# Pass 0 of a five-pass graph network: eight comparisons with a per-row scalar become two comparisons of whole tensors

## The reference

```
x = layernorm(x + L0(x))   # h = relu([x[src], edge_attr] @ W1a + b1a); h @ W1b + b1b; mean over the edges of each target; two dense layers
x = layernorm(x + L1(x))   # sum of x[src] * rsqrt(deg_out[src]) over the edges of each target, * rsqrt(deg_in), dense, batch norm
x = layernorm(x + L2(x))   # mean of x[src] over the edges of each target, dense, elu
x = layernorm(x + L3(x))   # two weighted relational convolutions, 4 relations
```

## Time and profile before

| | us |
|---|---|
| Median of three runs | 4328.8 |
| Profiled execution, its own time | 4328.8 |
| Its span | 4327.0 |
| GpSimd busy in the span | 3052.1 (71%) |
| TensorE busy, matmul | 2871.7 (66%) |
| VectorE busy | 1770.1 (41%) |
| ScalarE busy | 803.5 (19%) |

### The profile page before, as it was taken

The page is one execution under the profiler, slowest core; times in us unless marked ns, Lnnn a source line. Parts: engine busy times, 40 slices in busy tenths (PEclk is TensorE's granted clock), DMA queues, the critical chain, the costliest instruction groups (busy, mean ns, idle before and its releaser), DMA issues.

```text
span 4327.0 us, 54093 instructions
## 1 busy us (share of the span) xinstructions
PE 2871.7 (66%) x18556; PEld 2377.0 (55%) x18556; DVE 1770.1 (41%) x6259; ACT 803.5 (19%) x1557; POOL 3052.1 (71%) x3155
## 2 busy tenths in 40 slices
PE   5999999999889997999844444444443333333333
PEld 5888888888767775666533333433332333333333
DVE  7888888888752226333411111111111222121221
ACT  1445444444431113112200000000000000000000
POOL 4777777777347773777467777777767777777776
PEclk8999999999999997999855555555555555555555
DMA  6666676666556764777422222222221111111111
GB/s 206 216 212 211 211 218 211 211 215 209 172 149 199 202 199 124 222 222 225 134 61 66 62 66 62 66 66 62 62 62 54 56 54 56 53 55 54 56 55 51
DMA packets 413092, 556.43 MB, mean 129 GB/s; under 512 B 67041, under 2 KB 287969, under 8 KB 412545
## 3 DMA queue, kind: packets, MB, share of 16 engines
q0 software_dynamic: 114112, 262.48, 21.2%
q1 hardware_dynamic: 277184, 264.23, 19.8%
q10 hardware_dynamic: 21506, 26.10, 1.8%
HBM read 450.01 MB, written 102.55 MB: 128 GB/s over the span
## 4 chain that ended last, share of the span: by engine, by line
POOL 21%; PE 14%; DMA 9%; issue 7%; ACT 0%; DVE 0%; POOLq 0%; ACTq 0%; DVEq 0%; SPq 0%
POOL work L528 21%; PE bank L1134 13%; DMA work<-table_rel,reli 9%; PE bank L1743 0%; DMA table_rel<-work 0%; ACT work L1755 0%; ACT work L1815 0%; PE bank L1792 0%; DVE X L1876 0%; POOLq L95 0%; PE bank L1741 0%; ACTq L1819 0%; POOLq L595 0%; DVE work L1166 0%; PE bank L1988 0%
## 5 line engine op out<-in xcount | busy, mean ns | idle before, releaser
L528 POOL DMA_INDIRECT work<-table_rel,reli x1664 | 1612.5, 969 | 573.0 <-issue 461.3
L1134 PE MATMUL bank<-work 128*128 128x72 f32 x3328 | 750.8, 419 | 1259.6 <-DMA work<-table_rel,reli 1259.6
L1134 PEld LDWEIGHTS bank<-work 128*128 128x128 f32 x3328 | 708.9, 324 | 1323.5 <-DMA work<-table_rel,reli 1323.5
L528 POOL DMA_INDIRECT work<-table_pre,srci x832 | 805.8, 968 | 269.7 <-issue 267.8
L1116 DVE TENSOR_TENSOR acc<-acc,bank 128x72 f32 x208 | 47.8, 230 | 1749.5 <-PE bank L1134 1749.5
L1062 PE MATMUL bank<-work,acc 128*128 128x360 f16 x2574 | 437.9, 317 | 30.3 <-DVE acc L1204 18.0
L764 PE MATMUL bank<-w1a,work 128*128 128x256 f32 x1664 | 441.3, 391 | 17.7 <-DVE work L729 8.7
L528 POOL DMA_INDIRECT work<-table_mean,srci x312 | 303.7, 973 | 168.7 <-issue 87.5
L776 PEld LDWEIGHTS bank<-work 128*128 128x128 f32 x3328 | 399.5, 194 | 6.9 <-ACT work L863 2.2
L776 PE MATMUL bank<-work 128*128 128x64 f32 x3328 | 401.0, 275 | 1.6 <-ACT work L863 1.5
L528 POOL DMA_INDIRECT work<-table_gcn,srci x312 | 295.9, 948 | 109.7 <-issue 94.8
(11 more groups left out here) (264 smaller groups left out, 3201.8 us busy)
## 6 DMA issues: line engine op xcount, KB each, us to landing
work<-adj SPq DMA_DIRECT2D x104, 720.0 KB
adj<-X SPq DMA_DIRECT2D x130, 450.0 KB
work<-ea_cols SPq DMA_DIRECT2D x208, 256.0 KB, 3.0
work<-adj SPq DMA_DIRECT2D x52, 810.0 KB
work<-table_rel,reli POOLq DMA_INDIRECT x1664, 2.5
work<-table_pre,srci POOLq DMA_INDIRECT x832
table_rel<-work ACTq DMA_DIRECT2D x25, 512.0 KB
table_rel<-work SPq DMA_DIRECT2D x25, 512.0 KB
```

The costliest lines, as they stand in the source:

```text
L528: pool.indirect_dma_start(into[:, u, :], None, tables[p], bass.IndirectOffsetOnAxis(ap=idx_of(p)[:, t:t + 1].bitcast(U32), axis=0)).then_i ...
L1134: mm = pe.matmul(bank[4 + n % LATE_BANKS][:, 0:PAIR_WIN], late_gat[n % LATE][:, u, :], late_hot[:, n % LATE_HOTS, u * PAIR_WIN:(u + 1) * P ...
```

## The change

In `one_hot`, the function that makes the three one-hots of a group in pass 0, the four comparisons for `hot` (L648) give way to a call of `one_hot_of`, which the other passes use: one comparison of 128x256, of the tensor `iota` with the tensor `local`. The four comparisons for `hot_hi` (L651) give way to one comparison of 128x200, of `iota` (32-bit, where it was the 16-bit `iota_b`) with `src_hi`. The four for `hot_lo` stay. What is written is the same.

```
-            for u in range(U):
-                dve.tensor_scalar(hot[:, hq, u * WIN:(u + 1) * WIN], iota[:, 0:WIN], local[:, bass.ds(g * U + u, 1)], None,
-                                  ALU.is_equal)
-            for u in range(U):
-                dve.tensor_scalar(hot_hi[:, hq, u, :], iota_b[:, 0:NT], src_hi[:, bass.ds(g * U + u, 1)], None, ALU.is_equal)
+            one_hot_of(dve, g, hot[:, hq, :])
+            dve.tensor_tensor(hot_hi[:, hq, :, :], iota[:, 0:NT].unsqueeze(1).broadcast_to([P, U, NT]),
+                              src_hi[:, bass.ds(g * U, U)].unsqueeze(2).broadcast_to([P, U, NT]), ALU.is_equal)
```

## The result

The kernel after takes 4352.2 us (4350.6 to 4355.0), the kernel before beside it 4329.6: ratio 1.0053, 95% interval 1.0039 to 1.0067. It is slower by 22.6 us. I had forecast 4336.8 (+8), with a range up to 4347.

The account below looks back on a forecast made before the run. The prediction took GpSimd's gather instruction time to bound pass 0, with VectorE able only to stretch gathers. Terms -0.5 + 8 + 0.5 = +8 us on 4328.8 gave 4336.8 us, range 4327 to 4347.

Parts of the forecast that it names:

- What bounds pass 0: Pass 0: everybody follows GpSimd's gathers, median 946 ns plus a 0.30 us gap; VectorE can move only 18.3 us of stretches.
- VectorE's own time: Pass 0: VectorE saves some 0.65 us a group, 135 us in the pass, hidden behind GpSimd; value 0.
- What leaves: Pass 0: gather stretch under the removed L648 and L651 goes; 0.5 us off, 9.0 us at most.
- The mechanism: A gather reads indices 0.13 us in; a two-SBUF-input instruction stops that read from about 0.15 us after its start to its end.
- What comes: Pass 0: the two new comparisons stretch gathers; equal chance gives 9.8 us, bounds 5 and 14, taken as 8.
- The stretches of L677 itself: Pass 0: a faster VectorE can only change the phase of the L677s; +0.5 us, bounds -3 and +4.
- The stages behind: Stages after pass 0 are only shifted and keep their length.
- Rival B: Pass 0: reads are stopped from a comparison's first moment, or the phases meet; +20 us, 4349; chance 0.1.
- A: Pass 0: the phases miss, so the comparisons stretch almost nothing; +1 to +3 us, 4331; chance 0.24 together with D.
- C: Pass 0: all one-input comparisons hold gathers, eight go and the two new ones miss; 9.0 us faster, 4319.8; chance 0.06.
- D: Pass 0: VectorE gets ahead of TensorE and L677 waits more for its buffer; 0 to +2 us, counted with A.
- The range: Whole kernel: 4327 to 4347 us, reaching to A below and half way to Rival B above; forecast's own 4333 to 4343.

Follow-up runs that it names:

- e4: Kernel after, but both new comparisons read their row of numbers from PSUM, with the wait for that bank moved ahead of them: 4329.8 us, ratio 0.9999.
- e4c: Control for e4: kernel after with only the earlier wait for the bank, the row still in SBUF: 4350.5 us, ratio 1.0051.
- e1: Kernel before with only the first half of the change, one 128x256 comparison for hot; the four for hot_hi stay: 4338.6 us, ratio 1.0022.
- e2: Kernel before with only the second half of the change, one 128x200 comparison for hot_hi; the four for hot stay: 4333.3 us, ratio 1.0013.
- e3c: Kernel after with hot_lo's four comparisons moved between the two new ones: 4340.0 us, ratio 1.0021.
- e11: Kernel before; in passes 3 and 4 the 128x576 comparison reads its row from the just-emptied PSUM bank, ordered add, multiplication, comparison: 4291.8 us, ratio 0.9909.
- e7c: Kernel before; in passes 3 and 4 the 128x576 comparison, in its old place, reads its row from PSUM after a wait for TensorE: 4340.1 us, ratio 1.0024.
- e5c: Kernel after with each group's code comparisons (L675) moved behind the next group's one-hots: 4351.4 us, ratio 1.0045.
- e6: e4 with each code comparison cut into two halves, eight in place of four: ratio 1.0007 beside a kernel before that took 5031 us.

## Why the prediction was wrong

It named the right place, the right mechanism for one instruction by itself and the right sign, and mis-sized one term by two: what the two comparisons cost, 8 us forecast and 15.5 measured. Another 3 us came where 0.5 was forecast, by the same omission.

*What bounds pass 0.* Right. GpSimd's median of 946 ns and its gap stayed; 17.8 us more busy time are the 17.9 us of the pass.

*VectorE's own time.* Right: 417 and 357 ns (420 and about 360), the busy time of the whole span down by 121 us (144), more wait for landings, 244 us (about 250), and all of it worth nothing.

*What leaves.* Right in size: -0.8 us (-0.5), though 0.35 of it is only the first gather, which in after is counted under L640.

*The mechanism.* The read at 0.13 us, the hold to the end of an instruction with two SBUF inputs: e4 against e4c shows it, and e1 and e2 pay the equal-chance price, 5.6 + 3.9 = 9.5 us for 9.8.

*What comes: the step that failed.* "I take 8: a little under equal chance, because the comparisons stand behind L729 and L677, and a gather that L677 has held back just before has its next read 1.25 us later, past both comparisons, which are over after 0.7 us." Measured were 15.5 us, above the upper bound of 14 too. Two things are wrong in the sentence. The first is its unspoken assumption that a read held by the first comparison is let in at its end: 18 reads under the first were handed on to the end of the second, 5.0 us (after), none when the two stand apart (e3c, with 9.2 us of stretch under the comparisons). Of the 15.5, 0.35 are the pass's first gather, 5.0 this hand-on, and the other 10.2 what equal chance gives (9.8). The second is the phase. 1.25 us are counted from the end of the L677 that held the read, and there are up to three more L677 behind that one, at 0.37 us each; with two or three behind it the next read falls inside the comparisons, not past them. That gave the heaps, some 50 reads behind a held gather where the sentence expected none. They made little difference to the sum without the hand-on, because most of them fall late in L648 and cost 0.06 us. An even draw was the better guess than my reason for going below it, and the neighbour was the term I did not have.

*The stretches of L677 itself.* +0.5 forecast, +3.1 measured (17.1 to 20.1), inside the bounds of -3 and +4 but for another reason than the changed phase that I had in mind: it is the hand-on once more. Six reads under the last L675 were held past its end to the end of L648 (as at 920.49), 3.7 us beyond that end; without these the codes have 16.4. In e4c it is ten reads and 6.1 us of 21.9, in e1 ten and 3.4 of 20.3, in e3c eleven and 3.7 of 20.5, which leaves 15.8, 16.9 and 16.8. Where an instruction with one SBUF input follows the codes no read was handed on, and the codes have 17.1 (before), 16.0 (e2) and 16.2 (e4). So of the 17.8 us, 8.7 are hand-on.

*The stages behind.* Forecast 0. The profiled execution of after has +5.5 us there, e4c, e1, e2 and e3c have between -1.1 and +1.0 against before by the same reckoning, and e4 has -5.5, so this is the spread of one execution. The medians still differ by 22.6 us where pass 0 has 17.9; nearly 5 us are not placed.

*Rival B* gave 4349 and came nearest in time, but not by what it says: the first 0.15 us stayed free. An L640 in after that started 0.13 to 0.15 us ahead of a read met it without stretch four times (gathers at 484.96, 893.73, 1122.93 and 526.52 us), and it was L640 that grew, from 0.42 to 0.46 or 0.47. B blocks too early; what happens is that the block ends too late. A and C are refuted by e1 and e2, D by GpSimd's wait for TensorE, 2.1 us.

*The range.* The bounds of 5 and 14 came from instructions that stand alone or are followed by something that lets go. For two that stand back to back there was no row, and I didn't say so. Taking the pair as one hold, 0.69 us long (387.43 to 388.12) with 0.15 free, equal chance gives 0.54 x 0.54 / 2 / 1.25 = 0.117 us a group, 24 us: that belonged into the range as its upper end.

## What to carry to other kernels

Where GpSimd's indirect DMAs set the pace and VectorE has time to spare, as in this pass, fewer VectorE instructions are no gain, and one with two operands in SBUF beside them is a loss (22 us here); ask of every VectorE instruction whether an index read can fall into it, and what stands directly behind it. Two such instructions back to back can hold a read through both, so put short instructions with one SBUF input between them (e3c), or put one operand of each into PSUM, which removed the hold at the same duration (e4, e11). After such an edit look at the neighbours again: with every engine tied to the landings, moving one instruction by 0.6 us turned 11 meetings into 202 (e7c).

## What the runs showed of the hardware that I had not expected

- The hand-on. A held index read is not always let in when its holder ends; if the next VectorE instruction has already begun, the read can wait for that one too: 0.42 in place of 0.15 us with two instructions (387.57 in after), 0.79 us where it began under the codes (920.49), 1.0 us in e5c, 1.42 us with eight (e6). It is no certainty: at the same offset of 0.275 us, gathers of after took 1.09 (423.91, 662.18, 1056.10) or 1.37 (216.20, 455.28, 931.53). The traces say what goes with it. Of the reads 0.27 us into L640 in after and e4c, the 21 whose gather before had itself been held were all handed on, and the 12 others were all let in at L640's end; in e3c, with the one-input L649 behind L640, 18 followed a held gather and none was handed on. In the same way the reads 0.17 us before the end of the last code comparison that were handed on (6 in after, 10 in e4c, 11 in e3c, 10 in e1) all had a comparison with two SBUF inputs behind it, and the 37 at that place in before, e2 and e4, with one SBUF input behind it, were not. Why a held gather ahead matters stayed open.
- What holds a read is not only the number of SBUF inputs. The long one-input L677 does (17 us of before), under the short L648 and L651 of before 173 reads lost 0.8 us together, but in e5c, with the codes directly behind them, 119 reads under hot_lo's four lost 12.8 us. The section of the Trainium skill named above says that whoever starts first has the pair for the whole instruction. By that rule a read could not come between at all, and yet a comparison's first 0.15 us are free, in before and in after.
- An operand in PSUM costs these comparisons nothing: 417 and 354 ns with it, 417 and 357 without; 749 in e11 and 751 in before for 128x576.
- The Trainium skill, page "VectorE: DVE Perf Modes", section "Rules for kernel authors", advises a small count of operations. Here 1248 fewer instructions saved VectorE 121 us and cost the kernel 22.
